# A new order of work in layer 0, and one score bank moved from the exponentials to the maxima

## The reference

```
q, k, v = heads(x @ Wq.T), heads(x @ Wk.T), heads(x @ Wv.T)
q = q * cos + rotate_every_two(q) * sin          # k likewise
scores = q @ k.T * 16**-0.5, and -inf where the key is later than the query
out = softmax(scores) @ v
x = layernorm(x + out @ Wo.T)
```

## Time and profile before

| | |
|---|---|
| median of three runs | 1435.85 us |
| the profiled execution | 1435.74 us |
| its span, first to last instruction | 1433.9 us |
| mean granted TensorE clock | 0.943 of full |
| PE, DVE, ACT, POOL busy | 1202.5, 932.6, 602.6, 277.0 us |
| layer 0's score matmuls (L394), first and last start | 47.9, 603.7 us |
| first expert matmul | 668.48 us |

### The profile page before, as it was taken

One profiled execution on the slowest core, in us unless ns is written; L12 is line 12 of the kernel. 1 busy time (PEld: TensorE's weight loads), 2 busy tenths in 40 slices (PEclk: granted clock), 3 DMA queues, 4 the chain that ended last, 5 costly groups with the idle time before them and its releaser, 6 DMA issues. The chain is left out here.

```text
span 1433.9 us, 32422 instructions
## 1 busy us (share of the span) xinstructions
PE 1202.5 (84%) x12418; PEld 768.0 (54%) x12469; DVE 932.6 (65%) x2335; ACT 602.6 (42%) x1144; POOL 277.0 (19%) x294
## 2 busy tenths in 40 slices
PE   7579888889898889964999855999899999989854
PEld 3144545545454545543999733665656565555532
DVE  3676666666666666722777676777767677676732
ACT  1034444444444444532555312545455454545331
POOL 3111121111111120011111141213232322212022
PEclk9689999999999999996999978999999999999975
DMA  5341714141414131353422143451514334140000
GB/s 183 110 115 45 175 53 126 53 127 45 127 45 116 48 97 49 94 184 102 161 75 68 34 121 104 123 129 40 127 55 120 86 84 123 44 127 11 9 16 15
DMA packets 68264, 127.86 MB, mean 89 GB/s; under 512 B 8320, under 2 KB 58128, under 8 KB 64656
## 3 DMA queue, kind: packets, MB, share of 16 engines
q1 hardware_dynamic: 65040, 117.38, 29.2%
q0 software_dynamic: 3072, 8.41, 1.8%
HBM read 84.31 MB, written 40.66 MB: 87 GB/s over the span
## 5 line engine op out<-in xcount | busy, mean ns | idle before, releaser
L627 DVE TENSOR_REDUCE first_maxima<-bank 128x1 f32<-128x512 f32 (+3 forms) x352 | 220.6, 638 | 168.5 <-PE bank L397 167.2
L548 ACT ACTIVATE arena<-pair 128x512 f32<-128x512 f32 x320 | 187.3, 597 | 293.5 <-PE pair L426 291.5
L1473 ACT ACTIVATE second_probs<-pair 128x512 f32<-128x512 f32 (+1 forms) x256 | 135.3, 541 | 196.1 <-PE pair L1342 158.7
L394 PE MATMUL bank<-stacks 96*128 96x256 bf16 (+3 forms) x512 | 130.5, 312 | 39.5 <-DVE first_maxima L627 37.7
L1633 DVE TENSOR_REDUCE second_maxima<-bank 128x3 f32<-128x480 f32 (+1 forms) x160 | 105.2, 660 | 59.4 <-PE bank L1309 57.3
L373 PE MATMUL bank<-first_xT,w_qkv 128*128 128x512 f32 x256 | 129.7, 638 | 13.0 <-DMA first_xT<-in_xT 7.9
L419 PE MATMUL pair<-stacks 128*128 128x128 bf16 (+3 forms) x461 | 104.0, 295 | 0.9 <-ACT arena L548 0.5
L394 PEld LDWEIGHTS bank<-stacks 96*128 96x128 bf16 x512 | 45.1, 100 | 89.0 <-DVE first_maxima L627 59.1
L769 POOL TENSOR_TENSOR first_halves<-first_halves 128x512 f32<-128x512 f32 x32 | 41.5, 1296 | 264.4 <-DVE first_halves L612 264.4
L397 PE MATMUL bank<-constants_bf 128*128 128x128 bf16 (+2 forms) x352 | 88.7, 252 | 0.0
L1334 PE MATMUL pair<-second_q_stack,second_k_stack 128*32 128x160 bf16 (+4 forms) x2048 | 83.5, 230 | 3.2 <-ACT second_probs L1473 3.0
(11 more groups left out here) (337 smaller groups left out, 2406.7 us busy)
## 6 DMA issues: line engine op xcount, KB each, us to landing
stacks<-parked SPq DMA_DIRECT2D x96, 256.0 KB, 5.0
parked<-first_parts SPq DMA_DIRECT2D x32, 384.0 KB, 2.8
second_q_stack<-parked SPq DMA_DIRECT2D x48, 256.0 KB, 5.2
second_k_stack<-parked SPq DMA_DIRECT2D x48, 256.0 KB, 8.2
parked<-second_parts SPq DMA_DIRECT2D x30, 384.0 KB, 2.6
expert_xs<-sorted_x SPq DMA_DIRECT2D x39, 128.5 KB, 2.1
sorted_y<-expert_ys SPq DMA_DIRECT2D x39, 128.0 KB, 1.7
first_xT<-in_xT SPq DMA_DIRECT2D x8, 512.0 KB, 4.2
```

The source lines that it names most:

```text
L394: pe.matmul(mx[n % 2][:, x * wide:(x + 1) * wide], q[0:ROWS, i * GH + hh, qt * P:(qt + 1) * P], k[0:ROWS, i * GH + hh, 0:wide], start=(x = ...
L548: act.activation(PT[:, s:s + len(heads), lo:lo + each], ex[n % 3][:, 0:len(heads) * each].rearrange("p (h q) -> p h q", h=len(heads)), ACT ...
L627: dve.tensor_reduce(nm[:, i, qt, heads[0]:heads[0] + len(heads)], mx[n % 2][:, 0:wide].rearrange("p (h k) -> p h k", h=len(heads)), AX.X, ...
L1473: act.activation(PT[:, s:s + len(heads), lo:lo + each], scores[:, :, 0:each], ACT.Exp, scale=SCALE).then_inc(lp["exps"], 1)
```

## The change

A table `SHIFTED` is added, with a small shift of the sort time for 25 kinds of items, some of them by part (59 entries). `schedule0` adds it to an item's time before sorting; items that have a time from `front0` keep it. In SP's list of 121 items 13 places hold another item (the load of `x` stands ahead of a `park`), and POOL's order is as before. On PE the exponentials stand one place earlier among the maxima, the two halves of `values` stand next to each other behind `exp` 2, the second `qk` of a pair stands behind `exp` 3 or `turn`, the first `qk` of a batch's last pair stands among the last units of group 1, and `turn_a` stands behind `exp` 9. On DVE `rest` and `lo` stand some units later and the `stats` stand among the last maxima.

The maxima get the bank that the third exponential had: they take their number modulo 3 and wait for the one three before; the exponentials take theirs modulo 2 and wait for the one two before.

```diff
--- before.py
+++ after.py
@@ -144,12 +144,27 @@
     return time
 
 
+SHIFTED = {
+    "add": {0: -0.032, 1: -0.093}, "exp": {None: -0.088}, "hi": {0: -0.04, 1: -0.079, 2: 0.027, 3: -0.079},
+    "lo": {0: 0.197, 1: 0.34, 2: 0.033, 3: 0.228}, "logit": {None: 0.02}, "new": {0: -0.174, 1: -0.059},
+    "norm": {0: -0.02, 1: -0.024, 2: 0.006, 3: -0.055}, "o_in": {None: -0.049}, "park": {2: 0.277},
+    "qk": {(0, 0): 0.025, (0, 1): 0.025, (1, 0): 0.025, (1, 1): 0.025, (2, 0): 0.019, (2, 1): 0.08, (3, 0): -0.298, (3, 1): 0.025},
+    "rest": {0: 0.006, 1: 0.109, 2: 0.166, 3: 0.2}, "rope": {(0, 0): -0.084, (0, 1): -0.099, (1, 0): -0.07, (3, 1): -0.103},
+    "split": {None: 0.054}, "stats": {0: -0.063, 1: -0.067}, "sum": {0: -0.183, 1: -0.128, 2: -0.128, 3: -0.128},
+    "turn": {None: 0.078}, "turn_a": {0: 0.097, 1: 0.024}, "turn_o": {0: 0.024, 1: 0.013, 2: 0.014, 3: -0.024},
+    "turn_x": {1: 0.012}, "turned": {None: 0.006}, "v": {0: -0.023, 1: 0.069}, "v_in": {1: 0.029}, "values": {0: 0.037},
+    "x_in": {0: -0.079, 1: -0.063}, "xt": {None: 0.068},
+}
+
+
 def schedule0():
 
 
     plan, out, first = Causal, [], front0()
 
     def at(time, kind, b, i=0, j=0):
+        moved = SHIFTED.get(kind, {})
+        time += moved.get(None, moved.get((i, j) if kind in ("qk", "rope") else j if kind == "values" else i, 0))
         out.append((first.get((kind, b, i, j), time), len(out), kind, b, i, j))
 
     for b in range(B):
@@ -267,8 +282,8 @@
                             "m_dma2", "m_dma3", "c_ps", "exps", "pv_ps", "o_in", "o_ps", "a_ps", "y_ps", "var", "rstd",
                             "x_new", "xn_ps", "lg_ps", "read0", "read1", "dve_chain"] + [f"x{b}" for b in range(B)])
         read = [lp["read0"], lp["read1"]]
-        mx, wk = m["ps"][0:2], m["ps"][2:4]
-        ex = [m["pair"][0][:, 0:S], m["pair"][0][:, S:2 * S], m["pair"][1][:, 0:S]]
+        mx, wk = m["ps"][0:2] + [m["pair"][1][:, 0:S]], m["ps"][2:4]
+        ex = [m["pair"][0][:, 0:S], m["pair"][0][:, S:2 * S]]
         pv = m["pair"][1][:, S:2 * S]
 
         cst, red, gT = m["arena"][:, 0:flat], m["arena"][0:G0, flat:flat + D], m["arena"][0:G0, flat + D:flat + D + E]
@@ -386,14 +401,14 @@
                             pe.wait_ge(lp["consts"], 3)
                         if i == 0 and j == 0:
                             pe.wait_ge(lp[f"stack{b % 2}"], 192 * (b // 2 + 1))
-                        if n >= 2:
-                            pe.wait_ge(lp["s_max"], n - 1)
+                        if n >= 3:
+                            pe.wait_ge(lp["s_max"], n - 2)
                         qt, heads = plan.MAX[j]
                         wide = (qt + 1) * P
                         for x, hh in enumerate(heads):
-                            pe.matmul(mx[n % 2][:, x * wide:(x + 1) * wide], q[0:ROWS, i * GH + hh, qt * P:(qt + 1) * P],
+                            pe.matmul(mx[n % 3][:, x * wide:(x + 1) * wide], q[0:ROWS, i * GH + hh, qt * P:(qt + 1) * P],
                                       k[0:ROWS, i * GH + hh, 0:wide], start=(x == 0), stop=True, skip_group_check=True)
-                        o = mx[n % 2][:, 0:len(heads) * wide].rearrange("p (h k) -> p h k", k=wide)
+                        o = mx[n % 3][:, 0:len(heads) * wide].rearrange("p (h k) -> p h k", k=wide)
                         ins = pe.matmul(o[:, :, wide - P:wide], m["idb"][:, :], spread(m["mS0"][:, :], P, len(heads)),
                                         start=False, stop=True, skip_group_check=True)
                         ins.then_inc(lp["s_ps"], 1)
@@ -409,20 +424,20 @@
                             pe.wait_ge(lp[f"m_dma{i}"], 48 * (b + 1))
                             if b < 2 and i == 0:
                                 pe.wait_ge(lp["k_set"], GH * (b + 1))
-                        if n >= 3:
-                            pe.wait_ge(lp["exps"], n - 2)
+                        if n >= 2:
+                            pe.wait_ge(lp["exps"], n - 1)
                         heads, tiles = plan.EXP[j]
                         lo = 0
                         for hh in heads:
                             for kt in tiles:
                                 wide = S - kt * P
-                                pe.matmul(ex[n % 3][:, lo:lo + wide], k[:, i * GH + hh, kt * P:(kt + 1) * P],
+                                pe.matmul(ex[n % 2][:, lo:lo + wide], k[:, i * GH + hh, kt * P:(kt + 1) * P],
                                           q[:, i * GH + hh, kt * P:S], start=(lo == 0), stop=True, skip_group_check=True)
                                 lo += wide
                         if len(tiles) == 2:
-                            o = ex[n % 3][:, 0:2 * P].rearrange("p (r c) -> p r c", c=P)
+                            o = ex[n % 2][:, 0:2 * P].rearrange("p (r c) -> p r c", c=P)
                         else:
-                            o = ex[n % 3][:, 0:lo].rearrange("p (r c) -> p r c", r=len(heads))[:, :, 0:P]
+                            o = ex[n % 2][:, 0:lo].rearrange("p (r c) -> p r c", r=len(heads))[:, :, 0:P]
                         ins = pe.matmul(o, m["idb"][:, :], spread(m["mT0"][:, :], P, len(heads) * len(tiles)), start=False,
                                         stop=True, skip_group_check=True)
                         ins.then_inc(lp["c_ps"], 1)
@@ -546,7 +561,7 @@
                             act.wait_ge(lp["pv_ps"], behind + 1)
                         s = slot(b, i, heads[0])
                         act.activation(PT[:, s:s + len(heads), lo:lo + each],
-                                       ex[n % 3][:, 0:len(heads) * each].rearrange("p (h q) -> p h q", h=len(heads)),
+                                       ex[n % 2][:, 0:len(heads) * each].rearrange("p (h q) -> p h q", h=len(heads)),
                                        ACT.Exp, scale=SCALE).then_inc(lp["exps"], 1)
                     elif kind == "o_in":
                         act.wait_ge(lp["pv_ps"], NG * b + i + 1)
@@ -625,7 +640,7 @@
                         qt, heads = plan.MAX[j]
                         wide = (qt + 1) * P * len(heads)
                         dve.tensor_reduce(nm[:, i, qt, heads[0]:heads[0] + len(heads)],
-                                          mx[n % 2][:, 0:wide].rearrange("p (h k) -> p h k", h=len(heads)),
+                                          mx[n % 3][:, 0:wide].rearrange("p (h k) -> p h k", h=len(heads)),
                                           AX.X, ALU.max, negate=True).then_inc(lp["s_max"], 1)
                     elif kind == "split":
                         dve.wait_ge(lp["s_max"], NMAX * (NG * b + i + 1))
```

## The result

| | before | after |
|---|---|---|
| median, lowest to highest | 1436.38 (4 runs, 1433.95 to 1438.61) | 1362.20 (4 runs, 1359.35 to 1365.99) |
| profiled execution, span | 1435.74, 1433.9 | 1360.18, 1358.4 |
| ratio | | 0.9486, 95% interval 0.9454 to 0.9517 |

The change saves 75.6 us between the two profiled executions and 74.2 between the medians; I had forecast 50, and a range of 25 to 62. Lines of `kernel.py` behind the new table are 15 higher than before, so L394 is now L409, L419 is L434, L452 is L467.

A forecast was written before the change was run, and what follows sets the result against it. PE was taken to bound layer 0's batches of 74.5 us, waiting 9.9 us in each. Gains of 8.65 less 0.5 per batch over six batches gave -49, with the ends -50: 1386 us, range 1374 to 1411.

The forecast's parts named there:

- Step (7): Layer 0's ends: nothing up to about 100 us; after 607 us -2.3 for an x transpose's wait, +1.2 for exponentials, net -1.
- Step (5): Cost of only two exponential banks: 0.5 us per batch in the groups other than group 1, bounds 0 and 3.6.
- (1): Group 1 of a batch: four PE waits, 2.45 us, shrink to 0.3 through late rest and three maxima banks; gain 2.15.
- (4): Group 0: waits of x transpose and v product gain 1.3 us, the rank product 0.5, a maximum behind it 0.65.
- step (6): Queues: later lo, park, stack loads and send stay hidden with 3 us to spare; POOL's order unchanged; values now together, nothing.
- (2): Group 2: first output transpose gains 1.0 us, attended-row transposes 1.5, with rest and one maximum behind the norm.
- (3): Group 3: the output product's bank wait and two waits for maxima go; gain 1.55 us per batch.
- A: Rival, chance 0.15: DVE standing for POOL's pass brings PE waits back, 3.1 of 8.15 us per batch lost; 1405 us.
- B: Rival, chance 0.07: two exponential banks make ACT the gate, +4 us per batch, slower than before; 1460 us.
- C: Rival, chance 0.05; its sign was a granted clock below 1.00 between 136 and 450 us.
- D: Rival, chance 0.03, placed beyond the range's high end of 1411 us; the text given does not say what it claimed.

The follow-up runs named there:

- order_only: The new order with the banks of the kernel before (two for the maxima, three for the exponentials): 1371.87 us, ratio 0.9566 to the kernel before.
- values_split: The changed kernel with only the value products moved back, their two halves apart again: 1369.61 us, ratio 0.9556 to the kernel before.
- sends_first: The changed kernel with group 2's send ahead of the second stack loads and the rank product one exponential and maximum later: 1398.1 us, ratio 0.9752 to the kernel before.
- old_two_two: The kernel before, in its old order, with two banks for maxima and two for exponentials, the eighth bank unused: 1434.82 us, ratio 0.9999.

## Why the prediction was wrong, step by step

The direction and the mechanism in the steady state held; the sum was a third too small. Of the 25.6 us beyond the forecast some 11 lie ahead of batch 1's first maximum, 10.6 in the five batches, and the rest in the half batch behind the start, at layer 0's end and behind it.

**Step (7), the ends, failed.** I wrote that up to about 100 us DVE sets the pace, that its order is the same, and so "nothing". For the order that is nearly right: `order_only` reaches batch 1's first maximum at 108.17 us, before it was 109.45. For the bank it is wrong: the changed kernel reaches it at 98.07, and at 99.70 in its second profile, 10.1 and 8.5 us sooner than `order_only`. DVE does set the pace, but DVE itself stood 5.5 us for PE in 57 to 90 us of the trace of before, and PE for DVE; a third bank cuts such mutual waits. I read PE's waits at the start and never asked DVE's. How much of the 8.5 to 10 comes by way of the clock stays open: `values_split`, whose clock rose only at 68 us, reaches the place at 103.67, so 4.5 us ahead of `order_only`. The rest of the gain up to the first transposes, 5.4 us, is steady state, where the forecast had 4. At the other end step (7) had 2.3 us for the x transposes' wait; behind the last rows of output transposes above, the x transposes waited 7.8 us in all and wait 6.4.

**Step (5) and what I left standing in (1) to (4) were too dear.** I kept 0.3 (group 1), 0.1 and 0.3 (group 2), 0.6 (group 0) and 0.5 for the two exponential banks, 1.8 us per batch. Measured: 0.41 + 0.16 for the rank product, and nothing else in a clean stretch; too much by 1.2. The rule of 1.20 us for two exponentials on two banks against a pace of 1.02 may be right where it applies, but in the changed kernel's five batches PE was never shown waiting so.

**In step (6) "values ... nothing"** was 1.0 us per batch (`values_split`, and the starts on PE). I had counted these gaps as PE's own work; the floor of 64.6 was 0.8 too high for it, and with it the low end of the range. Together 2.2 per batch of the 2.5 between the 8.15 forecast and the 10.65 of a clean stretch. Against that stand the new waits for the send, 1.2 us in the five batches and 5.5 in all, where step (6) had 3 us to spare. It named the right queue: three of the four come where the send stands behind the six stack loads. The slack itself was some 1.5 us (`sends_first`).

The single terms: (2) right as a sum, and undoing either of its two moves brings 0.6 of the transposes' wait back; (3) right; (4) right, the rank's wait forecast at 0.45 as listed and measured at 0.41; (1) nearly right in size (2.15 forecast, all 2.45 gone) and wrong in cause, for the late `rest` was not needed.

**The rivals.** A did not come: DVE stands 0.7 us per batch for POOL's pass and no PE wait follows. B did not come either: the changed kernel has no listed wait for an exponential in five batches, and in the old order two exponential banks cost nothing that ten runs of `old_two_two` show. C: the granted clock was 1.00 from 140 to 450 us, two tight banks or not; the rule of the Trainium skill (TensorE: Matmul & The Clock Gate, "A second HAM failure mode: psum-queue depth-cycling"), that cycling through banks makes the clock swing, is not borne out by this trace. A longer stand does bring the clock down here, in `sends_first` behind 3.7 us (0.97 over 140 to 450 us). D is refused by 74 us.

## What to carry to other kernels

When every engine walks one written order, list the waits of the limiting engine in one period, add the part that the modelled matmul length hides, and ask for each which item stands ahead of it on the releasing engine: here moving items took away 10 of 74 us per batch with not one instruction less. Ask the same of the start, of both partners of each wait, for a mutual wait shows half of itself in either list. And try a spare buffer on the pair of engines that wait for each other: here it was worth some 14 us there, and between 0 and 5 on the other pair.

## What I had not expected of the hardware

TensorE's clock at the start could be raised from 0.71 to 0.91 of full over 33 us with fillers, and the time did not move by more than the runs scatter: with two banks a higher clock, bought with 30 fillers among the maxima, gained nothing. It is not worthless everywhere: with three banks and the same order, the clock at its lower level until 68 us instead of 64, and again at 85, cost 3.4 us. The same kernel's first transposes came at 135.45 and 137.08 us in two profiles, with the clock at its upper level from 62 us in one and from about 64 in the other; all kernels of the new order with two banks for the maxima came at 144 us or later.
